# Value products split over two halves of the queries, two transposes and two projection units moved to earlier steps, and seven maxima moved two units ahead in the feed-forward

## The reference

```
x = x + L0_attn(layernorm(x))     # 16 heads of 16; keys in blocks of 256, each block with its own row maximum
x = x + L0_ffn(layernorm(x))      # 256 -> 1024, relu, square, 1024 -> 256, ternary weights
x = x + L1_attn(layernorm(x))     # 16 heads of 16, softmax over all 512 keys, biases
x = x + L1_ffn(layernorm(x))      # 8 binary trees of 255 nodes, silu of the nodes on the chosen path
```

## Time and profile before

| | before |
|---|---|
| median of 3 runs | 3438.83 us |
| profiled execution, whole time | 3437.46 us |
| profiled execution, span | 3435.4 us |
| TensorE busy | 3023.4 us, 88% |
| VectorE busy | 2224.0 us, 65% |
| ScalarE busy | 1923.9 us, 56% |
| GpSimd busy | 909.4 us, 26% |
| mean granted TensorE clock | 0.938 of full |

### The profile page before, as it was taken

One profiled execution on the slowest core, in us unless ns is written; L12 is line 12 of the kernel. 1 busy time (PEld: TensorE's weight loads), 2 busy tenths in 40 slices (PEclk: granted clock), 3 DMA queues, 4 the chain that ended last, 5 costly groups with the idle time before them and its releaser, 6 DMA issues.

```text
span 3435.4 us, 48439 instructions
## 1 busy us (share of the span) xinstructions
PE 3023.4 (88%) x18980; PEld 1336.3 (39%) x18980; DVE 2224.0 (65%) x4099; ACT 1923.9 (56%) x2559; POOL 909.4 (26%) x1206
## 2 busy tenths in 40 slices
PE   0488899988999899988998889998899989998899
PEld 0124255242643326333362424524254232633336
DVE  0784866757566676766667486675856667576664
ACT  0274654737557474655746566474754737456474
POOL 0013223141321414113141232314132141321313
PEclk9589999999999899998999999999999989999899
DMA  3000000000100001000010000100001000100000
GB/s 116 21 21 19 21 26 32 21 19 21 40 27 12 25 16 50 27 2 29 24 38 27 20 21 22 36 21 19 21 29 39 12 19 21 46 28 5 29 18 19
DMA packets 92691, 90.88 MB, mean 26 GB/s; under 512 B 15757, under 2 KB 89877, under 8 KB 92453
## 3 DMA queue, kind: packets, MB, share of 16 engines
q1 hardware_dynamic: 92465, 87.79, 7.5%
HBM read 17.48 MB, written 8.39 MB: 8 GB/s over the span
## 4 chain that ended last, share of the span: by engine, by line
PE 64%; DVE 23%; ACT 5%; issue 2%; POOL 2%; SPq 2%; DMA 0%; DVEq 0%
PE ps L986 12%; PE ps L1053 12%; PE ps L1031 12%; PE ps L1231 8%; DVE nmax L748 8%; DVE nmax L751 7%; PE ps L1011 6%; PE ps L992 4%; PE ps L1202 3%; PE ps L1042 3%; ACT probs L524 2%; SPq L263 2%; PE ps L999 2%; PE ps L1222 1%; PE ps L1059 1%
## 5 line engine op out<-in xcount | busy, mean ns | idle before, releaser
L524 ACT ACTIVATE probs<-ps 128x1024 f32<-128x1024 f32 x1024 | 1043.1, 1025 | 398.1 <-PE ps L1042 390.1
L1031 PE MATMUL ps<-kst,qst 48*128 48x512 f16 x2048 | 751.8, 416 | 183.0 <-DVE nmax L748 77.9
L751 DVE TENSOR_REDUCE nmax<-ps 128x1 f32<-128x512 f32 x1024 | 651.0, 684 | 239.8 <-PE ps L1031 238.8
L748 DVE TENSOR_REDUCE nmax<-ps 128x2 f32<-128x512 f32 x1024 | 650.8, 684 | 219.4 <-PE ps L1031 215.5
L1042 PE MATMUL ps<-qst,kst 54*128 54x512 f16 x2048 | 725.9, 411 | 5.0 <-ACT probs L524 5.0
L1053 PE MATMUL ps<-probs,vn 128*32 128x512 f32 x4096 | 544.0, 604 | 6.6 <-ACT oT L512 6.6
L1031 PEld LDWEIGHTS ps<-kst,qst 48*128 48x128 f16 x2048 | 156.4, 94 | 870.8 <-DVE nmax L748 362.4
L420 POOL TENSOR_TENSOR probs<-probs 127x512 f16<-127x512 f32 (+1 forms) x256 | 292.2, 1162 | 519.7 <-ACT probs L650 519.7
L650 ACT ACTIVATE probs<-probs 127x512 f16<-127x512 f32 (+1 forms) x256 | 161.2, 630 | 350.5 <-DVE probs L940 346.9
L1231 PE MATMUL ps<-wout,probs 127*128 127x256 f16 (+1 forms) x3072 | 357.2, 273 | 0.0
L986 PE MATMUL ps<-hT,win 128*127 128x512 f16 (+1 forms) x1536 | 354.3, 380 | 2.6 <-ACT probs L626 2.6
(11 more groups left out here) (115 smaller groups left out, 3200.1 us busy)
## 6 DMA issues: line engine op xcount, KB each, us to landing
qst<-parts SPq DMA_DIRECT2D x384, 64.0 KB, 2.6
kst<-parts SPq DMA_DIRECT2D x384, 64.0 KB, 2.6
x<-in_x SPq DMA_DIRECT2D x16, 512.0 KB, 4.0
probs<-x SPq DMA_DIRECT2D x16, 512.0 KB, 3.0
out<-probs SPq DMA_DIRECT2D x16, 512.0 KB, 3.0
qst<-nrow SPq DMA_DIRECT2D x256, 12.0 KB
qst<-in_winT SPq DMA_DIRECT2D x1, 2040.0 KB
oT<-in_wfcT SPq DMA_DIRECT2D x1, 1024.0 KB
```

Of the source, the lines that this page charges most:

```text
L524: nc.scalar.activation(probs[:, g % 2, 2 * hf:2 * hf + 2, s % G, :], ps[:, 2 + 2 * hf:4 + 2 * hf, :], ACT.Exp).then_inc(exp_rd, 1)
L748: nc.vector.tensor_reduce(nmax[:, u, 2 * tt + half, :, slot], bank[tt % 2].rearrange("p (a s) -> p a s", s=BLK), AX.X, ALU.max, negate=Tru ...
L751: nc.vector.tensor_reduce(nmax[:, u, 2 * tt + half, 0, slot:slot + 1], bank[tt % 2], AX.X, ALU.max, negate=True).then_inc(max_rd, 1)
L1031: mm(bank[tt % 2], qst[lo:hi, ai % 2, e // 2, tt * P:(tt + 1) * P], kst[lo:hi, ai % 2, e // 2, :], start=True, stop=True).then_inc(max_ps, 1)
```

## The change

It has three parts.

1. Nine steps get their value product in two halves of the queries: columns 0 to 255 of all four heads between tiles 1 and 2, and columns 256 to 511 after tile 3, ahead of the side work. They are steps 4, 5, 9, 13 and 14 of phase 0, and 0, 1, 2 and 5 of phase 1. The same code serves layer 1, where steps 5, 9, 13 and 14 of phase 4 and 0, 1, 2 and 5 of phase 5 are split.
2. In phase 0 both transposes stand in step 0 (before: steps 1 and 2), the two low parts on VectorE in step 1 (before: 2 and 3), and the first two `qk_unit` in steps 2 and 3 (before: 3 and 4).
3. In the second feed-forward of layer 0 each pair of lead tiles stands two pairs sooner: pairs 0 and 1 ahead of the first `project`, and `project` 14 and 15 behind pairs 12 and 13.

```diff
-        T_BANK = {0: (7, 6), 1: (6, 7), 2: (1, 7), 3: (6, 7), 4: (0, 1), 5: (6, 7), 6: (1, 7), 7: (7, 6)}
-        Q_BANK = {0: (6, 7, 6, 7), 1: (7, 7, 7, 7), 4: (0, 1, 6, 7), 5: (7, 7, 7, 7)}
+        T_BANK = {0: (7, 6), 1: (7, 6), 2: (1, 7), 3: (6, 7), 4: (0, 1), 5: (6, 7), 6: (1, 7), 7: (7, 6)}
+        Q_BANK = {0: (6, 7, 6, 7), 1: (6, 7, 7, 7), 4: (0, 1, 6, 7), 5: (7, 7, 7, 7)}
...
+            def weighted(n, ai, g, kt, halves=(0, 1)):
+                if 0 in halves:
+                    if kt == 0 and not (ai == 0 and g == 0):
+                        pe.wait_ge(oT_sb, n * NG + g)
+                    if kt == 0 and g == 0:
+                        pe.wait_ge(v_sb, n * 2 + 2)
+                    pe.wait_ge(exp_rd, n * (2 * H) + (2 * (G * g + G - 1) + kt // 2 + 1))
+                lo, hi = halves[0] * (S // 2), (halves[-1] + 1) * (S // 2)
                 for j in range(G):
...
+                    i = mm(bank[6][32 * j:32 * j + 32, lo:hi], vn[:, ai % 2, kt, G * g + j, :], probs[:, g % 2, kt, j, lo:hi],
+                           start=kt == 0 and 0 in halves, stop=kt == T - 1 and 1 in halves, skip_group_check=True)
+                if 1 in halves:
+                    i.then_inc(pv_step, 1)
...
+                    split = s in ((4, 5, 9, 13, 14) if nxt == 1 else (5, 9, 13, 14))
+                    if s == G and nxt == 1:
+                        pe.wait_ge(qk_sb, (n + 1) * 4 + 1)
                     if s >= G:
-                        weighted(n, ai, s // G - 1, s % G)
+                        weighted(n, ai, s // G - 1, s % G, (0,) if split else (0, 1))
                     pair_of_tiles(b, ph, n, ahead, s, 1)
...
+                    if split:
+                        weighted(n, ai, s // G - 1, s % G, (1,))
+                    if s == 0 and nxt == 1:
+                        transposed(b, nxt, 0)
+                        transposed(b, nxt, 1)
+                    if s == 1 and nxt == 1:
+                        hT_read(b, nxt, 0)
+                        maxima_rows(n, 1)
+                    if s == 2 and nxt == 1:
+                        hT_read(b, nxt, 1)
+                        qk_unit(n + 1, nxt, 0)
+                    if s == 3 and nxt == 1:
+                        pe.wait_ge(mrow_sb, n * NG + 2)
+                        qk_unit(n + 1, nxt, 1)
...
+                    split = s in (0, 1, 2, 5)
...
                 lead_tiles(n2, 2, 1)
...
+                project(b, 8)
+                for c in range(11, UNITS):
+                    lead_tiles(n2, 2, 2 * (c - 11) + 2)
+                    hidden(b, c)
+                    lead_tiles(n2, 2, 2 * (c - 11) + 3)
+                    project(b, c - 2)
```

More of the change, by code:

```diff
@@ L535, in attention_even @@
                         row_read(*((n, (s + 3) // G) if s < 13 else (n + 1, 0)))
-                    if s in (1, 2):
+                    if s == 0 and nxt == 1:
+                        hT_high(b, nxt, 0)
+                        hT_high(b, nxt, 1)
+                    if s in (2, 3) and nxt == 1:
+                        qk_read(n + 1, nxt, s - 2)
+                    if s in (1, 2) and nxt == 5:
                         hT_high(b, nxt, s - 1)
-                    if s in (3, 4):
+                    if s in (3, 4) and nxt == 5:
                         qk_read(n + 1, nxt, s - 3)
@@ L806, in attention_even @@
                         normalise(b, 5)
-                    if s in (2, 3):
+                    if s == 1 and not l:
+                        hT_low(b, nxt, 0)
+                    if s in (2, 3) and l:
                         hT_low(b, nxt, s - 2)
@@ L811, in attention_even @@
                     maxima(*ahead, (2, 3))
+                    if s == 1 and not l:
+                        hT_low(b, nxt, 1)
                     if s == 0 and l:
@@ L1107, in attention_even @@
                         qk_unit(n + 1, nxt, 0)
-                    if s == 4:
+                    if s == 4 and nxt == 5:
                         pe.wait_ge(qk_sb, (n + 1) * 4 + 1)
@@ L1145, in attention_odd @@
                     pair_of_tiles(b, ph, n, ahead, s, 0)
[L1146 to L1149, removed]
+                    split = s in (0, 1, 2, 5)
+                    values_of = (n - 1, ai - 1, NG - 1, s) if s < G else (n, ai, s // G - 1, s % G)
+                    weighted(*values_of, (0,) if split else (0, 1))
                     pair_of_tiles(b, ph, n, ahead, s, 1)
+                    if split:
+                        weighted(*values_of, (1,))
                     if s == 1:
@@ L1312, in _ @@
                 hidden(b, 10)
-                project(b, 8)
                 lead = [(e, tt) for e in range(LEAD) for tt in (0, 2)]
@@ L1322, in _ @@
                 lead_tiles(n2, 2, 0)
-                hidden(b, 11)
                 lead_tiles(n2, 2, 1)
[L1325 to L1342, removed]
+                project(b, 8)
[4 more added lines that the diff above has]
+                    project(b, c - 2)
+                    if c == UNITS - 1:
+                        pe.wait_ge(qk_sb, n2 * 4 + 4)
+                        maxima_rows(n2, 0)
+                lead_tiles(n2, 2, 12)
                 project(b, 14)
-                lead_tiles(n2, 2, 11)
+                lead_tiles(n2, 2, 13)
                 project(b, 15)
[L1346 to L1349, removed]
                 attention_even(b, 4)
```

16 lines of the change are left out of this document (4 added, 12 removed).

## The result

| | before | changed |
|---|---|---|
| median | 3438.99 us (4 runs, 3438.67 to 3439.48) | 3383.15 us (4 runs, 3380.93 to 3384.19) |
| profiled execution, span | 3435.4 us | 3379.0 us |
| mean granted TensorE clock | 0.938 | 0.944 |

The account below looks back on a forecast made before the run. The bound was a round trip, TensorE and VectorE each waiting for the other. Terms 4.0+0+2.7 = 6.7 us a turn, 54 us over 8 turns, gave 3383.9 profiled, so 3385 predicted, 8 in 10 from 3372 to 3411.

Parts of the forecast that it names:

- The loop and its rules: Attention step: tile 1, whole product, tile 2, reduction, next tile 0, 3.09 us; five spacing rules for tiles, reductions and products.
- The price of a half product: Half a value product on TensorE costs 0.63 us, fixed part paid in full; bounds 0.55 and 1.09.
- Splits, 4.0 a turn: Split attention steps gain 2.0 us per pair of even and odd phases, two pairs in a turn.
- 0.33 more behind the second half: Split steps with maxima rows: the rows add 0.33 us after the second half, making the step 2.98.
- nothing gained, nothing lost: Moved transposes and units: steps 0 to 4 of phase 0 sum to 19.75 us, against 19.73 before.
- It rests on the clock rising after the first unit.: Phase 0: full clock by the second unit, in step 3; if later, 1.8 us lost in each turn.
- Clock late: Rival, chance 0.15: half clock of phase 0 lasts through both units; 4.9 us a turn, 3400 us.
- I take the middle, 2.7: Lead tiles in the second feed-forward gain 2.7 us a turn, between 2.0 and 3.5 if the half clock goes.
- What would show it: Signs included step 14 at 2.65 to 2.7 us; wrong if halves exceed 0.9 or half clock reaches step 4.
- Dear half: Rival, chance 0.10: a half product costs about 0.90 us; 2.8 us a turn, 3416 us.
- Half dearer than the whole: Rival, chance 0.04: array layout changes make a half product 1.20 us; 4.0 lost a turn, 3471 us.
- Lead gain given back: Rival, chance 0.12: TensorE waits before step 0 as long as before, lead tiles worth nothing; 4.0 a turn, 3407 us.

Follow-up runs that it names:

- e9: Changed kernel with the selection of tree 2 done four times over in each turn, same output; 3384.58 us, ratio 0.9846.
- e10: Changed kernel with the selections of trees 2 and 4 done four times over in each turn, same output; 3385.41 us, ratio 0.9849.
- e6: Changed kernel with the second half of each split product directly behind the first, between tiles 1 and 2; 3415.55 us, one run.
- e5: e4 with only plain steps split: 14 of phases 0 and 4, 0 and 2 of phases 1 and 5; 3393.92 us, one run.
- e2: Kernel before with the moved transposes and units alone, no product split; 3439.75 us, ratio 1.0003.
- e4: Changed kernel without the moved transposes and units, step 4 of phase 0 whole; 3369.80 us, ratio 0.9801.
- e3: Kernel before with the lead tiles two pairs sooner alone; 3413.69 us, ratio 0.9934.
- e11: Kernel before with the selection of tree 2 done four times over in each turn, as in e9; 3439.37 us, ratio 1.0002.
- e12: Kernel before with the lead tiles one pair sooner instead of two; 3424.34 us, ratio 0.9961.
- e7: Changed kernel with steps 8 and 12 of phases 0 and 4 split too, which carry long side work; 3383.99 us, one run.
- e1: Kernel before with the split steps alone, step 4 whole and nothing moved; 3387.96 us, ratio 0.9850.

## Why the prediction came out

The forecast held. Its mechanisms were right for parts 1 and 3, and its walk through part 2 failed. That it came within 2 us is luck in two ways: the misses are of opposite sign, and e9 and e10 show that 10 to 16 us of work can move the whole time by only 1 to 2, so a sum right to 2 us says little about its terms. The sections are the better test, and by them I go here.

- **The loop and its rules** held. Step 14 was foretold at 2.65 and is 2.66, its tile 2 at 1.19 and is at 1.17, step 15 at 2.85 and is 2.88. e6 shows the cause by taking it away.
- **The price of a half product**, "I take 0.63", is 0.665: step 14 less its 1.77 for tile 3 and 0.226 for the next tile. The fixed part inside a product is 0.24, where the working had 1.09 less twice 0.46, 0.17. The Trainium skill, page "TensorEngine Tiling (Array Packing)", section Key Properties, says that changing the tiling mode drains TensorE. e6 fits it, since the price is paid once for each stretch of products, but no run here shows that it is the drain that costs it; whatever it is, it is no more than 0.24.
- **Splits, 4.0 a turn**, were 4.5 (1.0 + 0.8 + 1.35 + 1.35). The term that was off most is "0.33 more behind the second half" for steps with rows. They take 2.86, not 2.98: 2.86 less 1.77, 0.665 and 0.226 leaves 0.20 for the rows. In the timeline above the rows' matmuls begin at 1431.64, while the half product of 1431.18 still runs (0.64). e5 shows that these splits pay. Two smaller ones: step 15 was 3.18 long before and not 3.1, so it gained 0.30 and not 0.25, and in phase 4 the split of step 9 gained nothing (2.97 and 3.20 before for steps 9 and 10, 2.96 and 3.21 now).
- **Part 2, "nothing gained, nothing lost"**, was +1.3 a turn. The step that failed is "It rests on the clock rising after the first unit." It rose after the second: step 3 took 5.20 and not 3.5, step 4 2.88 and not 2.65, and steps 0 to 2, at 12.97 and not 13.6, gave 0.6 back. The rows spoke against that step: in the earlier trace rows the half clock ended 16.8 after step 0, and by the prediction's own terms the second unit would begin 15.7 after it. The rival *Clock late* had the loss with 1.8 a turn. e2 shows that the moves alone cost nothing, e4 that beside the other parts they cost 13 us.
- **Part 3, "I take the middle, 2.7"**, was 3.7, just past its upper bound of 3.5. The idle times fell by 2.0, which is the 2.0 foretold (4.92 to 2.96), and the half clock did go, which by the middle I had counted at half its worth. e3 shows 3.6 alone. Of the stretch, 1.17 is the third `hidden`, at 1.47 again where it took 2.64.
- **The sum** of 6.7 stands against 6.9 measured. The 1.3 lost in part 2, which I had at nothing, is made up by 1.0 more from part 3 and 0.5 more from the splits, and that is luck.
- **What would show it**: two signs spoke against part 2. The unit in step 3 took 2.74 and not 1.47, and the half clock in phase 0 reached into step 4, which stood among the signs of being wrong. The other two of these signs stayed away: a half product takes 0.665, and the wait for `qst<-nrow` ahead of phases 1 and 5 did not come; step 0 of phase 1 waits 0.65 for a reduction, as before. VectorE's waits for tiles fell by 72 us (454 to 383), more than "some 30".
- The rivals *Dear half* and *Half dearer than the whole* are refuted by the 0.665, and *Lead gain given back* by e3.

What stays open is why the half clock of phase 0 begins 0.3 before step 0 in e2 and in the kernel before, and 1.4 to 1.9 after it in the changed kernel, and why it comes there in one piece in two turns and in two in five others. The runs show that it changes with where the work falls, and no more.

## What to carry to other kernels

When two engines wait for each other once a step, find the long instruction inside the loop, cut it, and put the second piece into the other engine's wait; the cut is worth its fixed price (0.24 us here) only in steps where TensorE idles, so leave alone those with long side work behind them (1.5 us here; the rows' 0.33 was short enough). Before you trust a term of a microsecond or two in a kernel that repeats a turn, look where the half clock stands in the turn: moving work shifts it, and gains and losses of that size come and go with it, so sum the sections and not the whole time. Run the parts of a change each alone and in pairs: here one of three was free alone and cost 13 us beside the others.

## What the hardware showed that I had not expected

- **In five kernels the turns settle on one of a few lengths.** The kernel before and e2 stand at 409.6 turn after turn, e3 and most turns of e6 at 406.2, the changed kernel at 402.7. The others do not settle: e11 and e12 alternate between two lengths, and e4 and e7 wander over 2.4 and 4.0 us. In settled kernels and in wandering ones added work can vanish: 9 of 10.5 us in e9, all of 10.4 in e11, and e7's longer steps, 10 us by their sections.
- **Stretches at half clock come and go with placement.** That of 3.4 in the second feed-forward followed TensorE's idle 1.81 in every turn and went away when pairs of tiles stood there (e3, the changed kernel), but e1 and e11 lost it in half of their turns without that. In the changed kernel the granted clock was full from 1388.10 to 1391.50 between two pieces at half clock, behind eight transposes in a row (1385.29 to 1387.26). The transposes don't explain it: the third turn has the same eight from 982.80 and no such gap, and so has e2.
- **Matmuls of 256 columns in float32** in four strips side by side take 391 ns each and eight of them 0.64, where eight of 512 take 1.06. Back to back, sixteen take 1.07.
